# Attention probabilities left unscaled, the PV result multiplied by spread reciprocals instead

## The reference, cut to what matters

```python
q = (x @ Wq.T) ...; k = (x @ Wk.T) ...; v = (x @ Wv.T) ...      # 32, 8, 8 heads of 128
q = _rmsnorm(q, q_norm_w); k = _rmsnorm(k, k_norm_w)
scores = jnp.einsum('bkgqd,bksd->bkgqs', qg, k) / math.sqrt(HD)
bias = jnp.where(rel > 0, NEG_INF, slopes[:, :, None, None] * rel)
attn = jax.nn.softmax(scores + bias[None], axis=-1)
out = jnp.einsum('bkgqs,bksd->bkgqd', attn, v)
s = out.reshape(...) @ Wo.T
x = x + s * _silu(ffn(xn))
```

## Time and profile before

| | us |
|---|---|
| median of 3 runs (1317.32 to 1318.14) | 1317.39 |
| profiled execution | 1317.9 |
| its span, first to last instruction | 1316.1 |
| TensorE busy | 1283.2 |
| VectorE busy | 974.1 |
| ScalarE busy | 651.2 |
| GpSimd busy | 689.7 |

### The profile page before, as it was taken

The page is one execution under the profiler, slowest core; times in us unless marked ns, Lnnn a source line. Parts: engine busy times, 40 slices in busy tenths (PEclk is TensorE's granted clock), DMA queues, the critical chain, the costliest instruction groups (busy, mean ns, idle before and its releaser), DMA issues. The chain is left out here.

```text
span 1316.1 us, 20988 instructions
## 1 busy us (share of the span) xinstructions
PE 1283.2 (98%) x7135; PEld 1102.1 (84%) x7135; DVE 974.1 (74%) x2087; ACT 651.2 (49%) x1425; POOL 689.7 (52%) x746
## 2 busy tenths in 40 slices
PE   8899999999999999999999999999999989999997
PEld 7788888888888888888888888888888878888886
DVE  6777787778777877787778777877788855555556
ACT  4555555555555555555555555555555523222222
POOL 3555564555455545554555455545565525555553
PEclk9899999999999999999999999999999999999999
DMA  3000000010000000100000000000020036445541
GB/s 121 18 16 17 33 17 17 17 33 16 18 16 33 17 17 17 33 17 17 17 33 17 17 17 33 17 17 17 17 65 25 1 93 180 128 128 128 128 128 65
DMA packets 29469, 57.89 MB, mean 44 GB/s; under 512 B 3648, under 2 KB 3648, under 8 KB 29248
## 3 DMA queue, kind: packets, MB, share of 16 engines
q1 hardware_dynamic: 29376, 56.68, 15.2%
HBM read 54.57 MB, written 2.10 MB: 43 GB/s over the span
## 5 line engine op out<-in xcount | busy, mean ns | idle before, releaser
L403 POOL TENSOR_TENSOR pb<-rel,coef 128x896 f32<-128x896 f32 (+1 forms) x255 | 292.0, 1159 | 128.0 <-PE T L957 120.6
L507 ACT ACTIVATE pb<-pb,low 128x1024 f32<-128x1024 f32 (+7 forms) x256 | 198.8, 777 | 190.4 <-DVE low L734 188.7
L497 ACT ACTIVATE pt_h<-T 128x512 fp32r<-128x512 f32 (+3 forms) x384 | 185.7, 486 | 117.5 <-PE T L957 114.1
L718 DVE TENSOR_TENSOR pt_l<-T,pt_h 128x512 fp32r<-128x512 f32 (+3 forms) x384 | 210.0, 550 | 42.6 <-ACT pt_h L497 42.6
L734 DVE CUSTOM_DVE_ANT_0 pb<-S,pb,ninv 128x1024 f32<-128x1024 f32 (+7 forms) x256 | 207.6, 811 | 39.7 <-PE S L979 34.6
L957 PE MATMUL T<-ident,pb 128*128 128x128 f32 x1152 | 190.8, 275 | 16.1 <-DVE pb L743 8.7
L957 PEld LDWEIGHTS T<-ident,pb 128*128 128x128 f32 x1152 | 141.6, 141 | 55.0 <-issue 15.2
L743 DVE TENSOR_SCALAR pb<-pb,rinv 128x1024 f32<-128x1024 f32 (+7 forms) x256 | 172.0, 672 | 9.0
L1011 PE MATMUL O<-pt_h,v_h 128*128 128x512 f32 (+2 forms) x384 | 140.6, 366 | 1.0 <-DVE pt_l L718 1.0
L976 PE MATMUL S<-kT_h,q_h 128*128 128x512 f32 x382 | 141.3, 370 | 0.0
L380 POOL TENSOR_TENSOR inv<-ms,cst 128x4 f32<-128x4 f32 x64 | 76.2, 1191 | 118.5 <-DVE ms L766 118.5
(11 more groups left out here) (165 smaller groups left out, 2880.5 us busy)
## 6 DMA issues: line engine op xcount, KB each, us to landing
wq_in<-in_wq SPq DMA_DIRECT2D x32, 256.0 KB, 2.8
wo_in<-in_wo SPq DMA_DIRECT2D x32, 256.0 KB, 2.6
stage<-in_wkv SPq DMA_DIRECT2D x8, 512.0 KB, 3.8
stage<-in_gate_w SPq DMA_DIRECT2D x14, 256.0 KB, 2.6
stage<-in_gate_z SPq DMA_DIRECT2D x14, 256.0 KB, 3.7
stage<-in_gate_s SPq DMA_DIRECT2D x14, 256.0 KB, 5.1
stage<-in_up_w SPq DMA_DIRECT2D x14, 256.0 KB, 5.3
stage<-in_up_z SPq DMA_DIRECT2D x14, 256.0 KB, 6.2
```

Of the source, the lines that this page charges most:

```text
L403: g_.tensor_tensor(pbuf(idx, t), rel[:, TOK - w:TOK], coef[:, t:t + 1].to_broadcast([P, w]), ALU.mult).then_inc(bias_ready, 1)
L497: a_.activation(pt_lot(pt_h, t, n), bank[:, 0:m * P].rearrange("p (k w) -> p k w", w=P), ACT.Copy).then_inc(tr_hi, 1)
L507: a_.activation(pbuf(idx, t), pbuf(idx, t), ACT.Exp, bias=low[:, idx:idx + 1], scale=-1.0, accum_out=rsum[:, idx:idx + 1]).then_inc(exps_r ...
L718: v_.tensor_tensor(pt_lot(pt_l, t, n), bank[:, 0:m * P].rearrange("p (k w) -> p k w", w=P), f(pt_lot(pt_h, t, n)), ALU.subtract).then_inc( ...
```

## The change

The probabilities are transposed as the exponential leaves them. VectorE takes the reciprocals of the row sums four tiles at a time (`reciprocals`), when all four exponentials of a query half are done. In the result O^T a query row is a column, so that its reciprocal is needed along the free dimension and in each of the 128 partitions: SyncE writes the four columns to a row of 512 numbers in a DRAM scratch, waits for it, and reads that row back into all partitions of `rb` (`spread`). VectorE multiplies O^T with `rb` into a buffer `o_f` (`v_scale`), which frees the O bank; ScalarE and VectorE split `o_f` as they split O before. The projections w0 to w3 of a head are done in the order of units 1, 0, 3, 2 and wait for the split of the half that they use.

```diff
+        def spread(h, c, freed):
+
+            n = v_no(h, c)
+            sp.wait_ge(rinv_ready, n + 1)
+            sp.dma_start(recips[n].rearrange("(t p) -> p t", p=P), rinv[:, c * CT:(c + 1) * CT],
+                         allow_slow_non_contiguous=True).then_inc(recips_out, 16)
+            sp.wait_ge(recips_out, n * 16 + 16)
+            if freed is not None:
+                sp.wait_ge(out_free, freed)
+            sp.dma_start(rb[:, :], recips[n:n + 1, :].to_broadcast([P, CH])).then_inc(recips_in, 16)
...
-                          accum_out=rsum[:, idx:idx + 1]).then_inc(exps_ready, 1)
+                          accum_out=rsum[:, t:t + 1]).then_inc(exps_ready, 1)
...
-            act.wait_ge(out_ready, at.n(name))
-            a_.activation(oT_h[:, j, cs], O[at.bank(name)][:, :], ACT.Copy).then_inc(out_hi, 1)
+            act.wait_ge(out_free, at.n(name))
+            a_.activation(oT_h[:, j, cs], o_f[:, :], ACT.Copy).then_inc(oT_hi, 1)
...
+                lot(h, 7, 0)
                 if prev:
                     v_hi(at, f"v0_{j}", (j - 1) % PER)
-                lots(h, 7)
+                lot(h, 7, 1)
...
-        def normalise(h, idx):
-            dve.wait_ge(exps_ready, h * QT + (idx + 1))
-            v_.reciprocal(rinv[:, idx:idx + 1], rsum[:, idx:idx + 1]).then_inc(rinv_ready, 1)
-            t = TILES[idx]
-            dve.wait_ge(rinv_ready, h * QT + (idx + 1))
-            v_.tensor_scalar(pbuf(idx, t), pbuf(idx, t), rinv[:, idx:idx + 1], None, ALU.mult
-                             ).then_inc(probs_ready, 1)
+        def reciprocals(h, c):
+
+            n = v_no(h, c)
+            dve.wait_ge(exps_ready, h * QT + (2 - c) * CT)
+            if n >= 2:
+                dve.wait_ge(recips_out, (n - 1) * 16)
+            cs = slice(c * CT, (c + 1) * CT)
+            v_.reciprocal(rinv[:, cs], rsum[:, cs]).then_inc(rinv_ready, 1)
...
+        def v_scale(at, name, h):
+
+            dve.wait_ge(recips_in, v_no(h, int(name[1])) * 16 + 16)
+            dve.wait_ge(out_ready, at.n(name))
+            v_.tensor_tensor(o_f[:, :], O[at.bank(name)][:, :], rb[:, :], ALU.mult).then_inc(out_free, 1)
...
-            pe.wait_ge(probs_ready, h * QT + (idx + 1))
+            pe.wait_ge(exps_ready, h * QT + (idx + 1))
...
-            pe.wait_ge(out_free, outputs)
+            pe.wait_ge(oT_ready, v_no(h0 + 1, c) + 1)
...
-                    project(at, f"w{n}_{j}", 4 * (j % 2) + n, h - 2 - j % 2, 0 if j >= 2 else 2,
-                            at.n(f"v0_{j - j % 2}"))
+                    project(at, f"w{n}_{j}", 4 * (j % 2) + (1, 0, 3, 2)[n], h - 2 - j % 2, 0 if j >= 2 else 2)
```

More of the change, by code:

```diff
@@ L195, in staging, with attention @@
     return loads, {"gate": col(0), "up": col(3)}
-def attention(nc, stack, keep, x, wq, wkv, wo, slopes, qkw, mats, down_sc):
+def attention(nc, stack, keep, x, wq, wkv, wo, slopes, qkw, mats, down_sc, recips):
     sb = lambda n, shape, dt=F32: stack.enter_context(nc.sbuf_tensor(n, shape, dt))
@@ L298, in _, with group @@
         sp.dma_start(keep["dsc"][:, :, :], down_sc).then_inc(keep["dsc_in"], 16)
-        def group(g, last=False):
+        def spread(h, c, freed):
[7 more added lines that the diff above has]
+            sp.dma_start(rb[:, :], recips[n:n + 1, :].to_broadcast([P, CH])).then_inc(recips_in, 16)
+        def group(g, kind):
+            at = Places(kind, g)
+            last = kind == "last"
             for j in range(PER):
                 h = g * PER + j
+                prev = not (kind == "first" and j == 0)
                 if last and j == 1:
@@ L315, in group @@
                     sp.dma_start(wq_in[:, :, :], wq[h + 1]).then_inc(wq_ld, 16)
+                if prev:
+                    before = at if j > 0 else Places(("first" if g == 1 else "steady"), g - 1)
+                    spread(h - 1, 0, before.n(f"v1_{(j - 1) % PER}"))
+                if not (last and j == PER - 1):
                     sp.wait_ge(wo_split, h + 1)
                     sp.dma_start(wo_in[:, :], wo[h + 1]).then_inc(wo_ld, 16)
+                spread(h, 1, at.n(f"v0_{j}") if prev else None)
         def ffn_load(i):
@@ L324, in ffn_load @@
                 sp.dma_start(s_i, s.to_broadcast([P, CH])).then_inc(ffn_ld[k], 16)
-        group(0)
+        group(0, "first")
         for g in range(1, GROUPS - 1):
-            group(g)
-        group(GROUPS - 1, last=True)
+            group(g, "steady")
+        group(GROUPS - 1, "last")
+        spread(HEADS - 1, 0, Places("last", GROUPS - 1).n(f"v1_{PER - 1}"))
         for k in ffn_in:
@@ L817, in group @@
             if kind != "first":
-                normalise(g * PER - 1, 7)
+                reciprocals(g * PER - 1, 0)
                 dve.wait_ge(kt_hi, g + 2)
@@ L828, in group @@
                 if prev and j > 0:
-                    normalise(h - 1, 7)
+                    reciprocals(h - 1, 0)
                 if j > 0:
@@ L861, in group @@
                 if w:
-                    project(at, f"w0_{j}", unit, kind == "first")
-                normalise(h, 2)
+                    project(at, f"w0_{j}", unit + 1, kind == "first")
                 if j == 2 and not last:
@@ L867, in group @@
                 if w:
-                    project(at, f"w1_{j}", unit + 1, kind == "first")
+                    project(at, f"w1_{j}", unit, kind == "first")
                 lot(h, 6, 1)
@@ L879, in group @@
                 else:
-                    project(at, f"w2_{j}", unit + 2, kind == "first")
+                    project(at, f"w2_{j}", unit + 3, kind == "first")
                 lot(h, 4, 0)
-                normalise(h, 4)
+                reciprocals(h, 1)
                 if w and more:
-                    project(at, f"w2_{j}", unit + 2, kind == "first")
+                    project(at, f"w2_{j}", unit + 3, kind == "first")
                 lot(h, 4, 1)
                 logits(h, 5)
-                normalise(h, 5)
                 if kind == "first":
@@ L899, in group @@
                     kv_copy(at, ["kv3"], 1)
-                normalise(h, 6)
                 lots(h, 2)
-                v_lo(at, f"v1_{j}", j)
+                v_scale(at, f"v1_{j}", h)
                 if w:
-                    project(at, f"w3_{j}", unit + 3, kind == "first")
+                    project(at, f"w3_{j}", unit + 2, kind == "first")
+                v_lo(f"v1_{j}", h)
                 logits(h, 7)
@@ L915, in _ @@
         epi = Places("epi")
-        normalise(HEADS - 1, 7)
+        reciprocals(HEADS - 1, 0)
         project(epi, "w1", 1)
@@ L1198, in _ @@
         epi = Places("epi")
[L1199 removed]
         def last_unit(name):
             unit = int(name[1])
[L1203 removed]
+            project(epi, name, unit, HEADS - 2, 2)
         last_unit("w1")
@@ L1569, in program @@
         with ExitStack() as stack:
-            attention(nc, stack, keep, x, wq, wkv, wo, slopes, qkw, {"gate": gate, "up": up}, down_sc)
+            recips = nc.dram_tensor("recips", (HEADS * NC, CH), F32, kind="Internal").ap()
+            attention(nc, stack, keep, x, wq, wkv, wo, slopes, qkw, {"gate": gate, "up": up}, down_sc, recips)
         with ExitStack() as stack:
```

35 lines of the change are left out of this document (18 added, 17 removed).

## The result

The changed kernel takes 1651.45 us (1650.60 to 1655.24, four runs), the kernel before beside it 1317.77. The ratio is 1.2528, with an interval of 1.2512 to 1.2543: 334 us slower, where 1305.1 was forecast. The direction is that of the first rival, the late trip, but some seven times its price.

What follows compares the result with a forecast made beforehand. TensorE, busy 98%, was taken to bound the kernel. Shorter waits summed to 12.35 us net, with the DRAM trip at 4.7 us hidden under its 7.4 limit, giving 1305.1 us against 1317.39; range 1299 to 1324.

Steps and rivals of the forecast that it cites:

- the first rival: The DRAM trip lands past its 7.4 us limit: slower, 1351 us at the upper bound; chance 0.20.
- What bounds: TensorE, busy 98% of 1316.1 us, bounds the kernel; only its idle stretches can be won.
- The gain of 12.35: TensorE's shorter waits across attention, summed by stretch, less new waits; 12.35 us won.
- VectorE's busy time: Over the whole kernel, VectorE loses 159 us of work and its busy time falls to about 815.
- second rival: Handovers before the low part of the output eat the gain: no change, 1314 us; chance 0.14.
- third rival: Fuller clock in the first head's stretch and shorter waits win more: 1300 us; chance 0.66 together with the forecast.
- The price of the trip, 4.7: Each DRAM trip: write 2.0 us, read 2.6, and 0.1 for SyncE to notice the reciprocal and landed write.
- The rule on descriptors: The trip's write becomes 512 pieces of 4 bytes; if that costs the upper row, the first rival holds, otherwise the sum.
- The limit of 7.4: In a steady head, the c=0 read may land up to 7.4 us after the reciprocal without cost.
- c=0 is the tight one: Half c=0 is tight: its reciprocals come at a head's end, its product early in the next; limit 7.4 us.
- One us late, one us lost: At 9.0 plus 0.1 us, 24 heads lose 1.7 each (41 us) and seven group starts 0.7 each (5).
- Loads have most of a head in hand: Weight loads on SyncE's queue, pushed by a trip, still have most of a head before they are needed.

Runs made afterwards that it cites:

- the constant kernel: Changed kernel without the DRAM trip, VectorE's product multiplying by a tile filled once with a constant (rows not normalised): 1309.56 us, ratio 0.9932.
- the logits first: Kernel with 16 B write pieces, a head's last logits moved ahead of the v1 output's low part: 1309.24 us, 0.9926; the fastest version normalising the rows.
- the lists: Three runs beside the constant kernel, timing unread writes to DRAM in several shapes: 8.7 us for 512 pieces of 4 B, 1.3 for 128 of 16 B.
- the unread trips: The constant kernel plus the changed kernel's write and broadcast read, into a tile that nobody reads: 1324.98 us, 1.0054.

## Why the prediction was wrong, step by step

- **What bounds.** Right: the gain could only come from TensorE's idle stretches. Without the trip the waits for L743 in the earlier trace rows (8.7 us) are gone, the low parts' 5.2 became 4.0.
- **The gain of 12.35.** Some 9 by the constant kernel. The attention part's end, TensorE's first gate matmul, came at 1070.22 against 1079.18. By the first exponentials of the heads, 4.0 us were won up to head 3 (some 4.7 forecast), 2.7 from head 4 to head 28 (3.0 forecast) and 3.4 behind it (4.2 forecast). Half of the shortfall lies in the step into the first new group: from head 3 to head 4 the constant kernel takes 34.67 us (129.44 to 164.11) against 33.47 (133.46 to 166.93), 1.2 lost where 0.5 was to be won. The low part ahead of the last logits there took 1.96 us and not the 0.65 it was priced at, beside a bias instruction of GpSimd, as in the row of "the logits first"; with the logits ahead of the low part that step took 32.90. The new wait for the low part of K was there: 1.7 us in 7. Its forecast, 0.37 each, is off by its own figures too: 555.34 - 555.03 is 0.31.
- **VectorE's busy time.** Forecast 815, measured 845. The terms nearly held (products 44.2, reciprocals 11.1): the drawn lengths of all its instructions add up to 151 us less than before, where 159 were forecast. The rest is in the drawing: a length overlaps the next start by some 0.08 (749.88 + 0.69 = 750.57, the next at 750.49), busy time counts that once, and with 384 fewer instructions the overlaps fell from 106 to 84 us.
- **The handovers (second rival).** They cost nothing that shows: the constant kernel has them all, and its waits for low parts are the 4.0 above.
- **More is won (third rival).** From 30 to 160 us the constant kernel's granted clock was 1.00, where the earlier trace rows has 0.97. But in the first 30 us it was 0.94, where the kernel before had 1.00, so that some 2 us were won (0.03 x 130 - 0.06 x 30). Whether the shorter waits did it isn't shown. (With levels of 1.2 and 2.4 GHz the 0.97 is some 8 us spent at the lower one; the prediction's 4 us are the work lost in them.)
- **The price of the trip, 4.7.** This step failed. The write was priced by the 256 KB store of outT, 2.0; it took 10.06 in a steady head, and SyncE waited 8.2 for it on the mean. The read was priced at 2.6 by wo; it took 3.3 in that head, 4.8 on the median. (The 0.1 for SyncE to notice has no row of before; in that head it issued the write 0.03 after the reciprocal's end.) Together 13.4, beyond even the upper bound of 9.0. The bound's row, qk_w with rows of 8 B at 5.3, was a load; no row of before had a small write, and two rows on loads and large stores bounded nothing.
- **The rule on descriptors.** The Trainium skill ("DMA: Bandwidth & Descriptors", Rules for kernel authors) warned of one descriptor per element. It was weighed as a price between the same two rows. It pointed the right way; but by the lists the count isn't what costs, since 128 such pieces 16 B apart took 1.2 us. Nor is it that a piece has under 512 B, the other line that the prediction quotes: 128 pieces of 16 B took 1.3.
- **The limit of 7.4.** Right, and the part of the working to keep: 13.4 - 7.4 = 6.0, TensorE's row says 6.06. The other heads near it show 5.75 and 5.99 at the same place, a group start 3.37. A trip of 5.3 us (1.43 to the read's issue, 3.9 for the read at the median, in the fastest version) costs next to nothing, one of 7.2 begins to.
- **c=0 is the tight one.** Right: it costs twice what c=1 does. But c=1 was given no limit at all, and alone it costs 108 us, by the O bank that its late product holds.
- **One us late, one us lost.** Too low in sum: 31 heads x 6.0 = 186 for c=0, measured 219. TensorE's idle time grew by less than that, 150, since group starts have more in hand, as the first rival said (3.37 above); busy time grew by 67 on top, which the prediction had at nothing. With both halves late it grew by 94.
- **Loads have most of a head in hand.** Wrong in the last group: 6.8 us of ScalarE for wq, once, by the unread trips.

## What to carry to other kernels

Price a transfer by a row of its own kind (direction, memory, piece), and where there is none, measure it alone before anything waits for it: a list of shapes fits into one run. Work the limit out first; if the unknown could pass it in every iteration, the loss is about the excess times the iterations, and here more through the clock. A round trip through DRAM within a head can be hidden, as it was here with 16 contiguous bytes for each partition and a product that doesn't come within 7 us of the reciprocals.

## What the runs showed of the hardware

- Writes to DRAM of 4 B pieces lying side by side: 7.6 us for 128 of them and 8.7 for 512 (medians), 1.2 us for 128 with 16 B spacing; four writes of 128 such neighbours into SBUF landed in 2.0 each.
- A broadcast of a 1 KB row from one SBUF partition to 128: 8.8 us for 128 KB, two in flight; from DRAM 256 KB in 3.9 to 4.8.
- VectorE's product of 128x512 in fp32: 691 ns with contiguous operands, 692 with one at a stride of two numbers, 1081 to 1085 at a stride of four.
- TensorE, with waits of up to 6.6 us at the low parts, had a mean granted clock of 0.93 in the middle groups, where the earlier trace rows has 1.00, and the same instructions took 94 us more.
